# Experts' Silu computed as a tangent and a VectorE multiply-add in a two-layer decoder kernel

## The reference

```python
x = x + _L0_attn_ref(_layernorm(x), Wqkv, Wo)          # 16 heads, rotary, causal
x = x + _L0_xattn_ref(_layernorm(x), ctx_2048)         # fp8-rounded product with the context
x = x + _L0_ffn_ref(_layernorm(x), Wg, W1, W3, W2, Ws1, Ws3, Ws2)
x = x + _L1_attn_ref(_layernorm(x), w_qkv, w_proj)     # int8 x ternary weights
x = x + _L1_xattn_ref(_layernorm(x), token_ids, ctx, ctx, ctx)
x = x + _L1_ffn_ref(_layernorm(x), w_gate, w_up, w_down, ln_weight)
```

```python
h = jax.nn.silu(jnp.einsum('td,eid->eti', xt, W1)) * jnp.einsum('td,eid->eti', xt, W3)
y = jnp.einsum('etd,te->td', jnp.einsum('eti,edi->etd', h, W2), combine)
z = jax.nn.silu(xt @ Ws1.T) * (xt @ Ws3.T) @ Ws2.T
```

## Time and profile before

| | us |
|---|---|
| median of 3 runs | 726.19 |
| lowest, highest | 725.18, 727.3 |
| the profiled execution | 725.6 |
| its span, first to last instruction | 723.7 |

### The profile page before, as it was taken

How to read it: one execution, slowest core, us unless ns; L and a number is a source line. 1 busy time by engine, 2 the same in 40 slices (tenths; PEclk the granted TensorE clock), 3 DMA queues, 4 the chain that set the end, 5 groups by cost and what they waited for, 6 DMA issues and landing times.

```text
span 723.7 us, 11688 instructions
## 1 busy us (share of the span) xinstructions
PE 527.7 (73%) x4689; PEld 362.9 (50%) x4716; DVE 471.7 (65%) x1049; ACT 343.7 (47%) x543; POOL 135.4 (19%) x142
## 2 busy tenths in 40 slices
PE   2663728527998789997789978999867677465775
PEld 1331414315676567675566756676645445233443
DVE  3667796796568864588645855458544664456985
ACT  2332416514772257822678226772478439213454
POOL 2225245350000400000040000004000040002543
PEclk9776768867999999999999999999989989769679
DMA  6032122201000010000000000001000000000000
GB/s 202 1 137 91 47 67 85 83 39 59 2 1 1 3 58 1 2 1 1 1 25 36 1 1 1 1 2 59 5 25 1 2 1 1 0 1 0 1 29 30
DMA packets 5706, 20.01 MB, mean 28 GB/s; under 512 B 879, under 2 KB 3055, under 8 KB 5012
## 3 DMA queue, kind: packets, MB, share of 16 engines
q1 hardware_dynamic: 5652, 19.26, 7.9%
HBM read 18.21 MB, written 1.05 MB: 27 GB/s over the span
## 4 chain that ended last, share of the span: by engine, by line
PE 42%; DVE 32%; ACT 14%; issue 8%; POOL 1%; DMA 1%; SPq 0%; ACTq 0%; DVEq 0%; POOLq 0%
PE ps L842 14%; PE ps L870 9%; ACT L1230 4%; DVE nmx L1555 4%; PE ps L627 4%; DVE hs L1670 3%; PE ps L737 2%; ACT hs L1230 2%; DVE hs L1664 2%; DVE y L1452 2%; PE ps L852 2%; PE ps L649 1%; PE ps L609 1%; DVE hl L1675 1%; ACT hh L1237 1%
## 5 line engine op out<-in xcount | busy, mean ns | idle before, releaser
L1237 ACT ACTIVATE hh<-hs 128x512 f16<-128x512 f32 (+1 forms) x68 | 42.0, 618 | 129.0 <-DVE hs L1670 129.0
L1664 DVE TENSOR_TENSOR hs<-hs,ps 128x512 f32<-128x512 f32 (+1 forms) x68 | 45.6, 670 | 81.0 <-ACT hs L1230 49.5
L487 POOL TENSOR_TENSOR ve<-mv,half 128x2 f32<-128x2 f32 x24 | 5.4, 224 | 344.7 <-DVE mv L1445 344.7
L1675 DVE TENSOR_TENSOR hl<-hs,hh 128x512 f16<-128x512 f32 (+1 forms) x68 | 49.3, 726 | 28.6 <-ACT hh L1237 28.0
L1555 DVE TENSOR_REDUCE nmx<-ps 128x2 f32<-128x512 f32 (+1 forms) x96 | 61.0, 680 | 3.8 <-PE ps L682 3.6
L870 PE MATMUL ps<-w2h,hh 128*128 128x256 f16 x200 | 55.8, 279 | 1.4 <-DVE hl L1675 1.3
L870 PE MATMUL ps<-w2l,hh 128*128 128x256 f16 x200 | 55.2, 276 | 0.0
L870 PE MATMUL ps<-w2h,hl 128*128 128x256 f16 x200 | 55.1, 276 | 0.0
L1230 ACT ACTIVATE hs<-ps 128x512 f32<-128x512 f32 (+1 forms) x68 | 39.6, 582 | 23.6 <-PE ps L842 23.2
L1670 DVE TENSOR_TENSOR hs<-hs,ps 128x512 f32<-128x512 f32 (+1 forms) x68 | 45.2, 665 | 1.1
L1230 ACT ACT_TABLE_LOAD x35 | 44.9, 1283 | 0.6
(11 more groups left out here) (245 smaller groups left out, 1352.3 us busy)
## 6 DMA issues: line engine op xcount, KB each, us to landing
stage<-in_w SPq DMA_DIRECT2D x12, 800.0 KB, 4.2
tstage<-in_tern SPq DMA_DIRECT2D x4, 1024.0 KB, 4.9
cs<-in_ctxT SPq DMA_DIRECT2D x1, 1024.0 KB, 10.1
out_x<-xs SPq DMA_DIRECT2D x4, 256.0 KB, 2.2
w0s<-in_w SPq DMA_DIRECT2D x1, 768.0 KB, 7.1
xs<-in_x SPq DMA_DIRECT2D x1, 768.0 KB, 8.4
lnwb<-in_lnw SPq DMA_DIRECT2D x1, 512.0 KB, 3.7
xs<-in_x SPq DMA_DIRECT2D x1, 256.0 KB, 2.7
```

Source lines behind the costliest of these rows:

```text
L1237: act.activation(hh[:, n % 2, 0:w], hs[:, n % 2, 0:w], ACT.Copy).then_inc(e_hi.sem, 1)
L1664: TT(hs[:, n % 2, 0:w], hs[:, n % 2, 0:w], ps[:, up_bank(n), 0:w], ALU.mult).then_inc(e_hb.sem, 1)
L1675: TT(hl[:, n % 2, 0:w], hs[:, n % 2, 0:w], hh[:, n % 2, 0:w], ALU.subtract).then_inc(e_lo.sem, 1)
```

## The change

The Silu of the 68 expert pairs becomes tanh(g / 2) on ScalarE. A new VectorE instruction, ahead of the product with the up bank, computes (tanh + 1) times the gate, which it reads from PSUM, and signals `e_gt`; the product waits for that signal. The factor 0.5 is put into the selection matrices, whose ones become halves. As the gate bank is now read by VectorE after ScalarE, the spread of a moe pair, which overwrites that bank, waits for `e_gt` in place of `e_sil`.

```diff
@@ selections @@
-        sel0[e, e * INTER:(e + 1) * INTER] = 1
-        sel0[16 + e, e * INTER:(e + 1) * INTER] = 1
-    sel0[32, E0 * INTER:MOE_ROWS] = 1
+        sel0[e, e * INTER:(e + 1) * INTER] = 0.5
+        sel0[16 + e, e * INTER:(e + 1) * INTER] = 0.5
+    sel0[32, E0 * INTER:MOE_ROWS] = 0.5
...
-        sel1[e, e * F1:(e + 1) * F1] = 1
+        sel1[e, e * F1:(e + 1) * F1] = 0.5
@@ TensorE, spread @@
                 if kind == "moe":
-                    pe.wait_ge(e_sil.sem, n + 1)
+                    pe.wait_ge(e_gt.sem, n + 1)
@@ ScalarE, silu_of @@
-                act.activation(hs[:, n % 2, 0:w], ps[:, gate_bank(n), 0:w], ACT.Silu).then_inc(e_sil.sem, 1)
+                act.activation(hs[:, n % 2, 0:w], ps[:, gate_bank(n), 0:w], ACT.Tanh, scale=0.5).then_inc(e_sil.sem, 1)
@@ VectorE, times_up @@
+                w = tiles_of(n) * S
                 dve.wait_ge(e_sil.sem, n + 1)
+                dve.scalar_tensor_tensor(hs[:, n % 2, 0:w], hs[:, n % 2, 0:w], 1.0, ps[:, gate_bank(n), 0:w],
+                                         ALU.add, ALU.mult).then_inc(e_gt.sem, 1)
+                dve.wait_ge(e_gt.sem, n + 1)
                 if n < ALL_MOE:
                     dve.wait_ge(e_b.sem, n + 1)
-                w = tiles_of(n) * S
                 TT(hs[:, n % 2, 0:w], hs[:, n % 2, 0:w], ps[:, up_bank(n), 0:w], ALU.mult).then_inc(e_hb.sem, 1)
```

More of the change, by code:

```diff
@@ L399, in decoder @@
         e_sil = sig("e_sil")
+        e_gt = sig("e_gt")
         e_hb = sig("e_hb")
```

## The result

| | before | after |
|---|---|---|
| median | 726.75 us (4 runs, 725.18 to 728.35) | 744.72 us (4 runs, 742.14 to 747.7) |
| the profiled execution; its span | 725.6, 723.7 | 743.6, 741.7 |
| mean granted clock of TensorE | 0.879 | 0.871 |
| ratio, 95% interval | | 1.0249 (1.0208 to 1.0289) |

The change costs 18.0 us, 2.5%; 13.1 us were forecast. Page of after: busy time by engine, the chain by engine and by line; before's is the earlier trace rows.

The account below looks back on a forecast made before the run. What TensorE, in its fixed order, waits for was taken to bound the kernel. Iterations 2 to 7, the last four pairs and the last stage summed to +13.1 us on 725.6: 738.7 us, range 730.5 to 745.5.

Parts of the forecast that it names:

- part 3: Spread now waits in VectorE's queue: at iterations 2 and 3, pair 8 costs 2.1 us and pair 9 another 1.6.
- term of pair 8: Iterations 2 and 3: spread moves from 322.83 to 328.8, behind the context's quantisation; turn of qq at 330.35, cost 2.1 us.
- C: Rival: longer waits put TensorE at 1.2 GHz more often, 0.5 to 1.7 us per stretch; four give 744; 12%.
- Pair 9: Iterations 2 and 3: spread waits for the multiply behind the router's picks, 3.8 us late, another 1.6 us each.
- rival B: Late spreads of pairs 8 and 9 mostly absorbed, half their cost not passed on: 732.5 us; 17%.
- Part 1: Loads at Exp and Silu go: spreads give back at most 6.8 us, 4.8 us in all over iterations 2 to 5.
- rival A: Faster: all 29 us of loads on the path, multiply exposed at some 20 pairs (14 us): 711 us; 5%.
- rival E: A table switch costs as much again as the load's own row, a drain: 724 us; 2%.
- Part 2: New multiply on VectorE: 0.69 us each, 0.72 with the product's wait; 47 us more busy, to some 72%.
- Part 4: Second expert layer: iteration 6 -1.4 us, iteration 7 -0.3, last four pairs +2.9 at 0.72 each.
- Part 5: Last stage keeps Silu: one load ahead of its first Silu, 0.5 us taken (bounds 0 and 0.6).
- Rival D: Tanh's table set lacks Exp, so the loads stay: 759 us; 2%.

Follow-up runs that it names:

- e9: Against after: a same-size multiply into a spare tile, gate factor left out, so the spread waits for ScalarE as before; 735.72 us, ratio 1.0116.
- e4: Against after: pair 8's multiply stands ahead of the context's quantisation in VectorE's queue; 737.92 us, ratio 1.0158.
- e8: Against after: 36 matmuls that nobody reads ahead of the spread of pair 8 in iterations 2 and 3; 743.46 us, ratio 1.02.
- e10: Against after: tangent and multiply only in pairs 0 to 5 of iterations 2 to 6, Silu in all others; 721.41 us, ratio 0.9901.
- e5: Against e4: pair 9's multiply too stands early, ahead of the router's picks; 741.45 us, ratio 1.0175.
- e1: Against after: tangent and halves without the new multiply, spread waits for ScalarE, gate factor left out; 711.5 us, ratio 0.9776.
- e2: Against before: one more multiply per pair into a spare tile ahead of the product; Silu, loads and the spread's wait stay; 753.71 us, ratio 1.0363.
- e3: Against before: the spread waits for a two-column VectorE operation in the new multiply's place; Silu and loads stay; 744.93 us, ratio 1.025.

## Why the prediction was right, and where it was not

**What bounds, and part 3.** Right. The waits appeared where they were named: 5.9 us ahead of the turn of qq (forecast 5 to 6), none at the turn, 2.5 at pair 9 (forecast 1.5). TensorE's waits on the spread are 32.1 us; e9 and after put 10 us on them (forecast 2 x 3.7 at pairs 8 and 9 of iterations 2 and 3, and a part of the terms of iterations 4 and 5).

**The term of pair 8 was mis-sized.** "The turn goes at 330.35", 2.15 us late, reckoned spread and downs at 2.4 GHz. Against the half iteration's start the turn came 3.9 us later than before: qq itself was 0.2 late, and the thirteen steps took 3.07 us at 1.2 GHz, not 1.53. The clock stood among the rivals (C: "each further stretch costs 0.5 to 1.7 us; four of them: +5, 744", 12%) and came in on top of the forecast. That the measured 744.7 is also C's number is luck in part: C had four further stretches of 0.5 to 1.7 us, and what is shown is one place with 3.0 us, while the last stage's 1.6 us over and the first stretch's 1.8 under are neither's. e4 gives 6.6 us for pair 8 of the two iterations where the sum had 4.2, and e8 shows the clock by itself, with the spread as late as in after: 3.0 us in iteration 3. The mistake was to weigh it as an alternative when the forecast itself lengthened the wait from 3.6 to 5.9 us ahead of twelve downs. Iteration 2 has the same wait, with 2.7 us more at 1.2 GHz and 5.2 us for the forecast 5.4. That is the piece in which before had lost time beside GpSimd; against e10's it is 10.3 us longer with 9.8 us more at 1.2 GHz, so the forecast was too low there as well.

**Pair 9 was overrated.** 1.6 us were counted in each of iterations 2 and 3; e5 takes 2 us of its wait away and gains nothing. That is what rival B says, at one of the two pairs it named; at pair 8 it fell with e4.

**Part 1.** The account of the spreads held (bound 6.8, e1 shows 6.1 less wait). The whole of the loads, 15.5 us by e1, is half of what rival A took from the chain's account (29), so A falls. Its own condition (fewer than 40 exposed multiplies) was met, since e2's 26.7 us are 26.7 / 0.72 = 37 of them; what was wrong in A is the 4% of the chain read as time to be had, and with 15.5 us the point of decision is 22 pairs. The first halves brought 2.6 us net where 4.8 were forecast, most of the shortfall in iterations 4 and 5. e9, in which the spread does not wait for the multiply, has 5.0 there, which points to that wait; it is a difference of 2.4 us over four pieces. Beside each load's own 1283 ns no drain is seen. The Trainium skill ("ScalarE: Activation LUTs", What ACT_TABLE_LOAD costs) puts about 1380 ns more on a switch; e1, which takes 68 away for 15.5 us in all, gives no sign of it on the path of this kernel, and rival E (724) falls.

**Part 2.** Right in size: 669 ns for 690, and the gap of two products 0.72. VectorE's busy time rose by 41.7 us where 47 were forecast. The multiplies are 45.5 (68 x 669 ns); the other 3.8 are instructions that before has stretched beside GpSimd (1.94, 2.26, 1.58 and 2.10 us in place of some 0.7 each, behind iteration 2's start) and after only once (1.90). The forecast share of 72% was taken on the old span; on the forecast one it is 70%, and 69% was measured.

**Part 4.** Right: -0.7 for -1.0, and +2.2 for +2.2. **Part 5.** The load costs 0.6, the upper bound (I took 0.5). Timeline of after at the last stage's first Silu:

```profile
675.76 0.60 ACT L1372 ACTIVATE fyT<-ps 128x512 f16<-128x512 f16 x1 [3.48 <-PE ps L1096]
676.38 1.28 ACT L1379 ACT_TABLE_LOAD   x1
677.68 1.26 ACT L1379 ACTIVATE fs<-ps,gg 128x512 f32<-128x512 f32 x2
```

The Silu stands right behind the load, and TensorE's second group of products there starts 2.95 us after the first in place of 2.33. The other 1.5 us of the last stage are in instructions that are the same in both kernels, and fit what such stretches differ by.

**Rival D** (the loads stay) falls with the two loads that are left.

## What to carry to other kernels

Before an operation goes from one engine to another, list who waits for its result and where the new instruction stands in its engine's order: here the move of a signal from ScalarE to VectorE's queue cost some 10 us, and moving one instruction ahead of a long chain took back some 6.6 (uncertain by 4). A table load is worth what the matrix engine waits behind it (15.5 us of 87 here), so trade it away only where two functions alternate (0.990 to 0.993, some of it from a piece that the loads don't touch) and not where the table stays in place (1.025 for all pairs). And when a forecast lengthens a wait of the matrix engine, reckon what runs behind it once at either clock: in iteration 3 the wait and the slow stretch were one event, not two cases. Last, before two traces are compared piece by piece, look in each for instructions that took longer than their form does elsewhere: one such piece of before changed by 5 us where nothing in the code had.

## What was not expected of the hardware

A VectorE operation can be stretched by GpSimd. In e3 the operation of two columns takes 0.17 us as a rule, and twice 1.86 us, beside a GpSimd instruction that ends at the same moment. Timeline of e3:

```profile
345.84 0.17 DVE L1663 TENSOR_SCALAR spare<-cst 128x2 f32<-128x2 f32 x1 [0.81 <-ACT hs L1232]
...
511.75 1.86 DVE L1663 TENSOR_SCALAR spare<-cst 128x2 f32<-128x2 f32 x1
511.68 1.90 POOL L528 TENSOR_SCALAR wt<-tstage 128x2048 f16<-128x2048 f32 x1
...
382.35 1.86 DVE L1663 TENSOR_SCALAR spare<-cst 128x2 f32<-128x2 f32 x1
381.75 2.44 POOL L524 TENSOR_SCALAR tstage<-tstage 128x2048 f32<-128x2048 f32 x1
```

In the first GpSimd's began 0.07 us earlier and both ended within 0.03 us; the spread of that pair waited 1.85 us for it. In the second both ended within 0.02 us, and the spread didn't wait; VectorE's queue was 1.7 us late. In before the same thing falls on the chain, at 245.49 and 250.56. The Trainium skill ("Trainium Architecture — The Big Picture", What this means for kernel authors) calls the ports that the two engines share an exclusive lock, not a split of bandwidth; the trace agrees for these two, with 1.86 us in place of 0.17.

The second thing is the pair of windows of after and e8 above: the same thirteen matmul steps at a granted clock of 0.50 after 5.9 us of waiting, and of 1.00 when 4.09 of them were filled with matmuls that nobody reads.
